# Opening of an attention and GRU kernel: bulk loads issued one a turn between value and key copies, first two inputs scaled together, first Newton steps on VectorE

## The reference

```
scale, shift = split(cond @ W_emb + b_emb)
xn  = rms_norm(x, g_norm) * (1 + scale) + shift          # per sequence
q, k, v = heads(xn @ W_qkv)                               # 16 heads of 16
o   = softmax(rms_norm(q, g_q) @ rms_norm(k, g_k)^T / 4) @ v
x   = x + o + o @ W_out
h   = cond;  for t in 0..31:  h = GRU(x[:, t], h; W_ih, W_hh, b_ih, b_hh);  y[:, t] = h
out = x + y
```

## Time and profile before

| what | value |
|---|---|
| median of 3 runs | 372.7 us (371.69 to 374.68) |
| profiled execution | 372.1 us |
| its span | 370.3 us |
| mean granted TensorE clock | 0.983 of full |
| busy: PE, DVE, ACT, POOL | 345.9, 263.2, 230.2, 206.0 us |
| chain that ended last, by engine | PE 75%, SP's queue 9%, DVE 6%, DMA 4% |
| DMA traffic | 24.88 MB |

### The profile page before, as it was taken

How to read it: one execution, slowest core, us unless ns; L and a number is a source line. 1 busy time by engine, 2 the same in 40 slices (tenths; PEclk the granted TensorE clock), 3 DMA queues, 4 the chain that set the end, 5 groups by cost and what they waited for, 6 DMA issues and landing times.

```text
span 370.3 us, 12367 instructions
## 1 busy us (share of the span) xinstructions
PE 345.9 (93%) x4334; PEld 308.2 (83%) x4334; DVE 263.2 (71%) x696; ACT 230.2 (62%) x668; POOL 206.0 (56%) x384
## 2 busy tenths in 40 slices
PE   8687899999999999999887999999999999999983
PEld 7465788878777887788676999999999999999982
DVE  3566999999999999999975555555555555555553
ACT  4566778777778777876644655556555556555452
POOL 5476777777777777777622444334444444444322
PEclk9898999999999999999998999999999999999998
DMA  6992332322222222223210000000000000000000
GB/s 197 340 315 69 86 85 79 83 79 80 78 71 74 79 79 66 80 79 84 81 39 2 2 30 28 30 28 28 19 9 28 28 28 28 28 28 28 28 31 28
DMA packets 20206, 24.88 MB, mean 67 GB/s; under 512 B 4162, under 2 KB 13012, under 8 KB 20180
## 3 DMA queue, kind: packets, MB, share of 16 engines
q1 hardware_dynamic: 19764, 23.75, 21.1%
q10 hardware_dynamic: 416, 0.79, 0.6%
HBM read 7.48 MB, written 4.19 MB: 32 GB/s over the span
## 4 chain that ended last, share of the span: by engine, by line
PE 75%; SPq 9%; DVE 6%; DMA 4%; issue 4%; ACT 1%; POOLq 0%; POOL 0%; DVEq 0%; ACTq 0%
PE bank L1004 34%; PE bank L1056 21%; PE bank L1150 4%; PE bank L1131 4%; PE bank L1119 4%; SPq L382 3%; PE bank L1111 2%; PE bank L1213 2%; SPq L346 2%; SPq L390 2%; DMA v_diag<-v_rows 2%; PE bank L1102 1%; DMA stage_w<-in_L_cond_W_qkv_dram 1%; DMA operands<-operands 1%; PE bank L1069 1%
## 5 line engine op out<-in xcount | busy, mean ns | idle before, releaser
L1056 PE MATMUL bank<-h,w_hh_sb 128*128 128x128 f32 x768 | 97.1, 275 | 1.5 <-DVE h L992 1.3
L1056 PEld LDWEIGHTS bank<-h,w_hh_sb 128*128 128x128 f32 x768 | 91.2, 191 | 2.3 <-DVE h L992 1.7
L977 DVE SCALAR_TENSOR_TENSOR operands<-bank,vec_cols,operands 128x128 f32<-128x128 f32 x64 | 22.3, 349 | 53.6 <-ACT operands L733 53.5
L733 ACT ACTIVATE operands<-bank,bsum 128x128 f32<-128x128 f32 x64 | 23.5, 367 | 57.2 <-PE bank L1056 53.0
L534 POOL TENSOR_TENSOR operands<-operands,h 128x128 f32<-128x128 f32 x64 | 29.3, 458 | 52.7 <-ACT operands L734 52.7
L1004 PE MATMUL bank<-pair_hi,wih_hi 128*128 128x256 f32 x180 | 52.7, 293 | 0.0
L1004 PE MATMUL bank<-wqkv_hi,xn_hi 128*128 128x256 f32 (+1 forms) x128 | 49.0, 383 | 2.9 <-ACT v_rows L614 2.5
L1004 PE MATMUL bank<-pair_lo,wih_hi 128*128 128x256 f32 x180 | 50.3, 279 | 0.0
L1004 PE MATMUL bank<-pair_hi,wih_lo 128*128 128x256 f32 x180 | 50.2, 279 | 0.0
L541 POOL TENSOR_TENSOR operands<-h,x2T 128x256 f32<-128x256 f32 x32 | 23.2, 725 | 41.3 <-issue 30.3
L1004 PE MATMUL bank<-wqkv_lo,xn_hi 128*128 128x256 f32 (+1 forms) x128 | 43.9, 343 | 0.0
(11 more groups left out here) (118 smaller groups left out, 869.7 us busy)
## 6 DMA issues: line engine op xcount, KB each, us to landing
v_diag<-v_rows SPq DMA_DIRECT2D x128, 34.0 KB, 1.9
operands<-operands SPq DMA_DIRECT2D x64, 64.0 KB, 2.0
operands<-operands SPq DMA_DIRECT2D x32, 128.0 KB, 2.0
out_dram<-operands SPq DMA_DIRECT2D x16, 256.0 KB, 2.0
x_in<-in_x_dram SPq DMA_DIRECT2D x7, 512.0 KB, 9.9
w_hh_sb<-in_L_cond_W_hh_dram SPq DMA_DIRECT2D x1, 768.0 KB, 10.0
stage_w<-in_L_cond_W_ih_dram SPq DMA_DIRECT2D x1, 768.0 KB, 10.9
w_emb_sb<-in_L_cond_W_emb_dram ACTq DMA_DIRECT2D x1, 512.0 KB, 4.6
```

The costliest lines, as they stand in the source:

```text
L733: act.activation(r_g[:, c, :], r_in, ACT.Sigmoid, bias=bsum[:, c:c + 1]).then_inc(r_ready[c], 1)
L977: dve.scalar_tensor_tensor(out=rh[:, c, :], in0=xnh[:, HN_COL:HN_COL + B], scalar=bhh[:, 2 * KC + c:2 * KC + c + 1], in1=r_g[:, c, :], op0 ...
L1056: last = pe.matmul(dst, gate(w_hh_sb, name, c)[k], moving, start=k == 0 and (name == "n" or opens and name == "z"), stop=k == KC - 1, skip ...
```

## The change

Five edits, all to the first 12 turns:

- SP loads the first two groups of x before cond.
- SP no longer issues the last four x loads, w_hh and w_ih ahead of the pipeline. spread_loads issues one of them at the end of each of its turns 5 to 10: four x loads, then w_ih, then w_hh.
- ACT scales group 1 right behind group 0, before it makes the second half of the high weight part and the second pair of roots.
- The first Newton step moves from POOL to DVE. DVE makes only the modulation scale before the first xmod; the modulation shift, both low weight parts and the key gains follow it (shifts_and_gains).
- PE runs the first group's six query and key products with the four of xn_hi first, and nine more filler transposes before them.

```diff
--- before.py
+++ after.py
@@ -44,6 +44,7 @@
 FIRST_NORMED = 4
 FIRST_PAIR = 2
 FIRST_LOOPED = 12
+FIRST_SPREAD = 4
 
 
 def adaptive_attention_gru(
@@ -178,6 +179,7 @@
         vec_ps = sem("vec_ps")
         vec_cols_ready = sem("vec_cols_ready")
         vec_ready = sem("vec_ready")
+        scale_ready = sem("scale_ready")
         mod_ready = sem("mod_ready")
         k_diag_clear = sem("k_diag_clear")
         parity_step = sem("parity_step")
@@ -345,8 +347,8 @@
             def load_x(lo, hi, loaded):
                 sp.dma_start(x_in[:, lo:hi, :], x_groups[:, lo:hi, :]).then_inc(loaded, 16)
 
+            load_x(0, FIRST_PAIR, x_first_loaded)
             sp.dma_start(cond_sb[:, :], cond).then_inc(cond_loaded, 16)
-            load_x(0, FIRST_PAIR, x_first_loaded)
             for row, vector in ((12, b_emb), (16, g_norm)):
                 n = vector.shape[0] // P
                 sp.dma_start(vec_rows[row:row + n, :], vector.rearrange("(n p) -> n p", p=P)).then_inc(vec_loaded, 16)
@@ -363,14 +365,19 @@
             sp.dma_start(stage_w[:, :, 2 * D:3 * D], qkv_chunks[:, :, 2 * D:3 * D]).then_inc(wv_loaded, 16)
             load_x(4, 8, x_loaded[1])
             sp.dma_start(stage_wo[:, :, :], w_out.rearrange("(c p) n -> p c n", p=P)).then_inc(wo_loaded, 16)
-            for i in range(2, 4):
+            for i in range(2, FIRST_SPREAD):
                 load_x(4 * i, 4 * i + 4, x_loaded[i])
-            sp.dma_start(w_hh_sb[:, :, :], w_hh.rearrange("(c p) n -> p c n", p=P)).then_inc(hh_loaded, 16)
-            for i in range(4, len(x_loaded)):
-                load_x(4 * i, 4 * i + 4, x_loaded[i])
-            sp.wait_ge(wqk_ready, KC)
-            sp.wait_ge(wv_ready, 1)
-            sp.dma_start(stage_w[:, :, :], w_ih.rearrange("(c p) n -> p c n", p=P)).then_inc(ih_loaded, 16)
+
+            def spread_loads(i):
+
+                if i < len(x_loaded):
+                    load_x(4 * i, 4 * i + 4, x_loaded[i])
+                elif i == len(x_loaded):
+                    sp.wait_ge(wqk_ready, KC)
+                    sp.wait_ge(wv_ready, 1)
+                    sp.dma_start(stage_w[:, :, :], w_ih.rearrange("(c p) n -> p c n", p=P)).then_inc(ih_loaded, 16)
+                elif i == len(x_loaded) + 1:
+                    sp.dma_start(w_hh_sb[:, :, :], w_hh.rearrange("(c p) n -> p c n", p=P)).then_inc(hh_loaded, 16)
 
             sp.wait_ge(k_diag_clear, 1)
             sp.wait_ge(ones_ready, 2)
@@ -398,6 +405,8 @@
                 g = group(base, u, SP_KEYS)
                 if g is not None:
                     place_keys(g, (u - SP_KEYS) % 2)
+                if isinstance(base, int) and SP_V <= base + u < FIRST_LOOPED:
+                    spread_loads(FIRST_SPREAD + base + u - SP_V)
 
             pipeline(sp, body, NG - 1 + max(SP_V, SP_KEYS))
 
@@ -494,16 +503,6 @@
             pool.wait_ge(threes_ready, 1)
             pool.wait_ge(ones_ready, 2)
 
-            first = [norm_first[:, i, 0:FIRST_PAIR] for i in range(7)]
-            pool.wait_ge(first_norm, 3)
-            pool.tensor_tensor(first[4], first[3], first[3], ALU.mult).then_inc(first_norm, 1)
-            pool.wait_ge(first_norm, 4)
-            pool.tensor_tensor(first[5], first[4], first[1], ALU.mult).then_inc(first_norm, 1)
-            pool.wait_ge(first_norm, 5)
-            pool.tensor_tensor(first[4], threes[:, 0:FIRST_PAIR], first[5], ALU.subtract).then_inc(first_norm, 1)
-            pool.wait_ge(first_norm, 6)
-            pool.tensor_tensor(first[6], first[4], first[3], ALU.mult).then_inc(first_norm, 1)
-
             def second_norms():
                 second = [norm_first[:, i, FIRST_PAIR:FIRST_NORMED] for i in range(7)]
                 pool.wait_ge(rs0_ready, LAG_QK)
@@ -575,9 +574,11 @@
                .then_inc(first_norm, 1)
             act.wait_ge(vec_ps, 1)
             act.copy(vec_cols[:, :], p_o[:, 0:20]).then_inc(vec_cols_ready, 1)
-            for c in range(KC):
+            def projection_weights(c):
                 act.wait_ge(qk_loaded[c], 16)
                 act.copy(wqkv_hi[:, c, 0:2 * D], stage_w[:, c, 0:2 * D]).then_inc(wqk_hi_ready, 1)
+
+            projection_weights(0)
 
             def second_norms():
                 act.wait_ge(x_loaded[0], 16)
@@ -702,9 +703,11 @@
                 if m is not None:
                     input_high_part(m, (u - ACT_XN) % 2)
                 n = group(base, u, ACT_XHAT)
-                if n is not None:
+                if n is not None and not turn_is(base, u, ACT_XHAT + 1):
                     scaled_input(n, (u - ACT_XHAT) % 2)
                 if turn_is(base, u, ACT_XHAT):
+                    scaled_input(1, 1)
+                    projection_weights(1)
                     second_norms()
                 if turn_is(base, u, ACT_XN):
                     value_weights()
@@ -766,28 +769,43 @@
                 dve.tensor_scalar(norm_first[:, 1, second], norm_first[:, 0, second], 4.0 / DH, 4.0 * RMS_EPS,
                                   ALU.mult, ALU.add).then_inc(ms4_ready, LAG_QK)
 
+            dve.wait_ge(threes_ready, 1)
+            first = [norm_first[:, i, 0:FIRST_PAIR] for i in range(7)]
+            dve.wait_ge(first_norm, 3)
+            dve.tensor_tensor(first[4], first[3], first[3], ALU.mult).then_inc(first_norm, 1)
+            dve.wait_ge(first_norm, 4)
+            dve.tensor_tensor(first[5], first[4], first[1], ALU.mult).then_inc(first_norm, 1)
+            dve.wait_ge(first_norm, 5)
+            dve.tensor_tensor(first[4], threes[:, 0:FIRST_PAIR], first[5], ALU.subtract).then_inc(first_norm, 1)
+            dve.wait_ge(first_norm, 6)
+            dve.tensor_tensor(first[6], first[4], first[3], ALU.mult).then_inc(first_norm, 1)
+
             def modulation():
 
                 dve.wait_ge(vec_cols_ready, 1)
-                dve.scalar_tensor_tensor(out=gqk[:, :], in0=gq_col, scalar=DH ** -0.5, in1=gk_col,
-                                         op0=ALU.mult, op1=ALU.mult).then_inc(vec_ready, 1)
-                dve.wait_ge(parity_step, 2)
+                dve.tensor_scalar(bemb1[:, :], bemb[:, 0:KC], 1.0, None, ALU.add).then_inc(vec_ready, 1)
+                dve.wait_ge(emb_ps, 1)
                 dve.wait_ge(vec_ready, 1)
-                dve.tensor_scalar(gqk_parity[:, :], parity[:, :], gqk[:, 0:1], None, ALU.mult).then_inc(vec_ready, 1)
-                dve.tensor_scalar(bemb1[:, :], bemb[:, 0:KC], 1.0, None, ALU.add).then_inc(vec_ready, 1)
-
-                projection_weights(0)
-                dve.wait_ge(emb_ps, 1)
-                dve.wait_ge(vec_ready, 3)
                 for c in range(KC):
-                    dve.tensor_scalar(mod_scale[:, c, :, :].rearrange("p g b -> p (g b)"), p_s[:, c * B:c * B + B],
-                                      bemb1[:, c:c + 1], gnorm[:, c:c + 1], ALU.add, ALU.mult)
+                    last = dve.tensor_scalar(mod_scale[:, c, :, :].rearrange("p g b -> p (g b)"),
+                                             p_s[:, c * B:c * B + B], bemb1[:, c:c + 1], gnorm[:, c:c + 1],
+                                             ALU.add, ALU.mult)
+                last.then_inc(scale_ready, 1)
+
+            def shifts_and_gains():
+
                 for c in range(KC):
                     last = dve.tensor_scalar(mod_shift[:, c, :, :].rearrange("p g b -> p (g b)"),
                                              p_s[:, (KC + c) * B:(KC + c) * B + B], bemb[:, KC + c:KC + c + 1], None,
                                              ALU.add)
                 last.then_inc(mod_ready, 1)
-                projection_weights(1)
+                for c in range(KC):
+                    projection_weights(c)
+                dve.scalar_tensor_tensor(out=gqk[:, :], in0=gq_col, scalar=DH ** -0.5, in1=gk_col,
+                                         op0=ALU.mult, op1=ALU.mult).then_inc(vec_ready, 1)
+                dve.wait_ge(parity_step, 2)
+                dve.wait_ge(vec_ready, 2)
+                dve.tensor_scalar(gqk_parity[:, :], parity[:, :], gqk[:, 0:1], None, ALU.mult).then_inc(vec_ready, 1)
 
             def projection_weights(c):
 
@@ -882,7 +900,7 @@
             def modulated(g, slot):
                 dve.wait_ge(xT_ps, g + 1)
                 if isinstance(g, int) and g == 0:
-                    dve.wait_ge(mod_ready, 1)
+                    dve.wait_ge(scale_ready, 1)
                 if later(g, 2):
                     dve.wait_ge(xn_ready, g - 1)
                 dve.tensor_tensor(xmod[:, slot, :].rearrange("p (c b t) -> p c b t", c=KC, b=GB),
@@ -942,6 +960,8 @@
 
                 if turn_is(base, u, 0):
                     modulation()
+                if turn_is(base, u, DVE_XMOD):
+                    shifts_and_gains()
                 if turn_is(base, u, DVE_XMOD):
                     second_norms()
                 if turn_is(base, u, DVE_XMOD + 1):
@@ -1075,10 +1095,23 @@
                                          stop=k == KC - 1, skip_group_check=True)
                 return last
 
```

(19 more changed lines are left out.)

## The result

The changed kernel takes 375.6 us (median of 4 runs, 374.95 to 378.23), the kernel before 372.2 in the same comparison: ratio 1.0111, 95% interval 1.0068 to 1.0155. It is slower by 1.1%. The forecast was 373.2, +1.1 us against the profiled execution before; the measured time lies inside the range, 369.8 to 376.0, but the cost came out as +3.4 us in the medians, three times what was forecast. The profiled execution took 376.15 us for a span of 374.3, 4.0 more than before's.

A forecast was written before the change was run, and what follows sets the result against it. SP was taken to bound until 45.92, then PE. First scores 29.4 + 2.9 = 32.3, plus 25.0 puts group 5 at 57.3 against 56.25, +1.1; 372.1 + 1.1 = 373.2 us, range 369.8 to 376.0.

The forecast's parts named there:

- the late cond: Opening: cond, issued after x, lands 2.45 us later, where x did, moving vec_cols from 8.18 to 10.63.
- its second price: Opening: PE's idle time brings the lower clock, costing 0 to 1.7 us; 1.1 taken, so vec_cols at 11.7.
- cond hardly late: Rival, opening: cond only 0.46 later, vec_cols 8.64, group 5 at 54.2, time 370.1 us; chance 0.20.
- The sign I had named for it: Opening: a granted clock near 0.5 after cond's transposes, which were to come at about 6.4.
- The first scores: PE's scores of group 0: 29.4 from shorter key copies plus 2.9 us of pipeline delay, 32.3 instead of 32.01.
- the gain of the spreading: First key copies: 1.86 us instead of 2.73, landing 2.04 later, so first scores at 29.44 instead of 32.01.
- the forecast's shift: Opening: the pipeline delayed 2.9 us, from xmod at 13.4 instead of 11.3 and 0.8 more to the second xn_hi.
- The turns: First scores to group 5: three x-load turns of 4.90 (4.35 + 0.55) and two of 5.17, 25.0 us.
- the weight turns: SP's turns with w_ih and w_hh: 4.35 + 0.8 = 5.15 us, hidden by PE's 5.17.
- The issue cost belongs to the size: Rival, SP's turns: 1.67 per x load, 2.13 per weight, first scores to group 5 31.0, time 379.2; chance 0.10.
- SP's issues are no bound: Rival, SP's turns: the five loads cost SP nothing, group 5 at 52.6, time 368.5 us; chance 0.07.
- The yardstick of the prediction: Scores of group 5, at 56.25 before: a shift there shifts the end; everything after costs and gives nothing.

The follow-up runs named there:

- e3: The changed kernel with cond issued ahead of x again; ratio to the kernel before 1.0050.
- e16: The changed kernel with cond first and all bulk loads ahead of the pipeline as before, so only the new opening; ratio to the kernel before 1.0030.
- e4: The kernel before with w_ih and w_hh issued by SP after the loop, in turns 32 and 33; ratio to the kernel before 0.9954.
- e5: e4 plus six unread loads in the turns where the change has its six, same rows, 64 bytes each; ratio to the kernel before 1.0068.
- e6: e5 with the six extra loads at full size, still read by nobody; ratio to the kernel before 1.0055.
- e14: e3 with one of four value copies of each of the first seven groups issued by ACT; ratio to the kernel before 1.0004.
- e12: e3 with one of four value copies of all 32 groups issued by ACT; ratio to the kernel before 1.0200.
- e13: e8 with the late weights and one of four value copies of each group issued by ACT; ratio to the kernel before 1.0143.
- e7: The edits of e3 and e4 together: new opening, cond first, x loads ahead, weights late on SP; ratio to the kernel before 0.9988.
- e8: e7 with DVE's second norms ahead of the two low weight parts; 368.7 us, ratio to the kernel before 0.9947.
- e15: e8 with one of four value copies of each of the first seven groups issued by ACT; ratio to the kernel before 0.9987.
- e2: The changed kernel with the bulk loads back ahead of the pipeline, x still before cond; ratio to the kernel before 1.0040.
- e1: The kernel before with only the loads spread over SP's turns 5 to 10; ratio to the kernel before 1.0063.
- e9: e3 with the six spread loads issued by ACT in its turns 5 to 10; ratio to the kernel before 1.0025.

## Why the prediction was right and wrong

**The opening: the late cond right, its second price unproven.** Cond lands late as chosen: its transposes at 5.79 (forecast 6.4), vec_cols 10.96 (11.7), xmod 12.60 (13.4). The rival "cond hardly late" had it 0.46 later only, and falls; e3 shows what the place is worth. The trace agrees here with the ring order that the Trainium skill states (DMA: Bandwidth & Descriptors, "Queues, rings and completion order"): cond, issued second, is used 1.80 us later. DVE's second norms came at xmod + 2.87 (2.6), the first xn_hi at xmod + 3.53 (3.4), the second at xmod + 6.95 (6.6). The second xn_hi is 2.39 late where 2.9 was forecast.

The price of PE's idle time looks near: the embedding products took 3.79 us and 2.54 before, +1.25 where I had put 1.1. But its cause is not shown. The sign I had named for it, a granted clock near 0.5, did not come; and in the kernels with cond first the same products took anything from 2.02 us to 3.75, the 3.75 in e16 with PE idle for only 0.19 us ahead of cond's transposes. That this term came out is as far as I know luck.

**The first scores: near, by errors that cancel in part.** 31.76 against 32.3. The 2.04 us of the earlier trace rows run from the start of the last key issue, 43.75, to the landing, and the 1.86 of the three issues (42.49 to 44.35) contain that issue of 0.59 as well: the sum counts it twice. Read without that, the landing is the same after the change: from 29.61, the start of the last issue, to 31.76 it is 2.15, and before 43.75 to 45.92 it is 2.17. Nor did the backlog make the 2.73 of the earlier trace rows: without bulk weights in the opening, and with its key issues at 25.70, e4 still has 2.67. One issue in it, at 26.72, was a long one of 1.54, of which more below; in the change the long one fell on a value copy just ahead, at 26.99, and the keys took 1.86. So the 1.86 was chance and not the gain of the spreading. No value copy of ACT waited for a landing, and key issues began at 28.34 (28.44 by the forecast's shift); this too is partly luck, since the opening was 0.5 less late than forecast and the long issue at 26.99, 1.31 us, filled the difference.

**The turns: wrong, and this is the step that failed.** Group 5 was forecast at 57.3, 1.1 late, and came at 59.33, 3.08 late. The prediction said "In the pipeline a turn of SP is four value copies (2.49) and three key copies (1.86), 4.35 us without a bulk load". It took the shortest key row of before. Over four turns of before SP has a mean of 4.75: 0.09 a turn are the two gaps between the groups of issues, and the rest is that the keys took 2.61 and 2.36 in two of the four, because single issues are longer. Two things follow. The x turns are not 4.90. They took 5.02, 5.23 and 5.59, 15.84 where 14.70 stood, +1.14. And the weight turns are not hidden by PE's 5.17: SP bounds these too (4.98 and 5.58, 10.56 against 10.34, +0.22), and the last keys held it for 2.89 where the first took 1.86 and landed a little later after their issue, +1.17. Together +2.5 of the 2.57 between 27.57 and 25.0. Three single issues make up most of it: those at 39.22, 51.06 and 56.01 took 1.17, 1.19 and 1.62 us where the usual one takes 0.59, 2.2 us more. With the mean turn the same sum is 5 x (4.75 + 0.62) = 26.9 us, and group 5 comes at 32.3 + 26.9 = 59.2. It was seen at 59.33, but from first scores 0.5 earlier and a stretch 0.7 longer, so that the closeness is in part luck.

```profile
37.31 0.60 SPq L390
...
37.95 1.32 SPq L390
...
39.31 0.60 SPq L390
```

These are the three key issues of before that together took 2.61, from its chain of waits. The traffic of before from 37.8 to 39.0 us holds one packet that no line of the kernel issued:

```profile
q8 instruction: 1, 0.02, 5.4%
```

It is a packet of 16 KB on a queue that the profile calls instruction, from 37.87 to 38.90. In the 17 profiles, between 20 and 200 us, 153 issues of SP last over 1.0 us, and every one of them overlaps such a packet; away from these packets no issue lasts over 0.85. Of the 203 packets in that stretch 50 pass without such an issue. Between 80 and 160 us, where the turns are a hardware loop, none of the 17 has such a packet, nor an issue over 0.7 us. So the long issues go with the loading of instructions while the turns are written out. That they are caused by it fits all of this and is not tested: no run changed the number of instructions alone. In the change the packets at 39.07, 50.71 and 56.08 are those of the three long issues above.

**The size of a load's issue: right.** 0.55 was taken for an x load, 0.58 and a gap of 0.05 were found; e5 has 0.59 a load. w_hh held SP for 1.19, but this is one of the long issues and not the size: in e3 the same issue took 0.58 and w_ih 0.53.

**The rivals.** "The issue cost belongs to the size" is refuted by e5 and e6: 64 bytes a row cost what full rows cost. Its place was right, though, and its sign: the five loads on SP, between keys and values, made the kernel slower. It was given 0.10 for another mechanism, with the loads 1.67 and 2.13 long. "SP's issues are no bound" is refuted by e5, which adds six issues with next to no bytes, and by e14, which keeps the loads and takes one issue a turn off SP. The Trainium skill (DMA: Bandwidth & Descriptors, "Issuing engines are not separate DMA queues") says that the time to start a transfer is usually small beside it. In this stretch it is not: a key copy is issued in 0.59 us and landed 2.04 after the start of that issue, and seven such issues fill SP's turn.

**What is left.** In the profiles, group 5 accounts for 3.08 of 4.0 us. Most of the rest, 0.8, arises in the last three turns of the attention, where the change does nothing. From g5 to the GRU single profiles of these kernels (e12 and e13 apart) scatter from 143.7 to 147.2 us, so it can't be told from chance. The yardstick of the prediction, a shift at group 5 is a shift of the end, is therefore rough: e7, e8, e14 and e15 have g5 earlier than before by 2.6, 3.9, 1.9 and 3.1 us, and their ratios give back only 0.4, 2.0, nothing and 0.5 us. Why is open, and so is e16, whose g5 is before's and whose ratio is 1.0030.

## What to carry to other kernels

Count the issues of a DMA queue, not the bytes: where seven or eight small copies a turn keep it busy, one more transfer costs a full issue, some 0.6 us here, whatever it carries, and it belongs ahead of the stretch, behind it, or on an engine that has time there. Take the mean turn over the whole stretch from start to start, since the shortest one leaves out the gaps and the long issues. Look at all queues of the profile when an issue is long, also those that the kernel does not use. And move work off the bound engine only for as long as it is the bound: the same move gained 2.7 us between g0 and g5 when it was made for seven groups (e14), and made for all 32 the kernel took 2% more than before (e12).

## What the runs showed of the hardware

The column of the granted clock and the durations of products do not always agree. Windows of after (PE, PEld, DVE, ACT, POOL busy, granted clock, DMA share, GB/s) behind the 2.22 us in which PE waited ahead of group 1's scores show a fall from 1.00 to 0.52, near 0.5, the level of 1.2 GHz:

```profile
36.00:38.00 2.00, 0.44 (x32) 0.43 (x32) 0.70 (x2) 0.65 (x3) 1.16 (x4) 1.00 0.66 201
38.00:40.00 2.00, 2.00 (x54) 1.65 (x37) 1.55 (x3) 0.37 (x1) 0.49 (x2) 0.52 0.57 177
40.00:42.00 2.00, 2.00 (x9) 1.71 (x8) 1.18 (x3) 1.51 (x4) 0.68 (x2) 0.62 0.40 114
```

But behind the idle time ahead of cond's transposes the column stays at 1.00, while the same 16 products need half as long again. The tile's rows (shortest/median/longest ns), after:

```profile
L1043 PE MATMUL bank<-h,w_emb_sb x16: 421/421/579, 6.9 to 10.3; 128*128 128x128 f32 x16
```

and before:

```profile
L1023 PE MATMUL bank<-h,w_emb_sb x16: 274/275/551, 5.4 to 7.7; 128*128 128x128 f32 x16
```

e2, with the same order of cond, has 421 too; e3 and e8, with cond first, 275. But e16, with cond first and PE idle for only 0.19 us there, has 421 as well, and e1 and e6, with no idle time there, have 366 and 392. So the durations, and not the clock column, tell what PE lost in the opening, and what makes them long is open.

An issue of SP takes 0.59 us in the turns for value copies of 34 KB, key copies of 64 and 128 KB and, within 0.01, x loads of 512 KB; it takes over 1.0 only beside a packet of 16 KB on the instruction queue. And a key copy of 64 KB took 5.54 us to land (e9), 1.89 of it its own issue, a long one, while a load of 768 KB was on its way from ACT's queue; the usual landing is 2.0.
